# Picked rows folded in four, four, five and six banks, with masks and factors in PSUM

## What is computed

```python
# L0: a matrix per edge from the edge's features
h = relu(edge_attr @ W1 + b1); weights = (h @ W2 + b2).reshape(-1, 16, 16)
out = segment_sum(einsum('ei,eio->eo', x[src], weights), dst) + x @ root
# L1: two convolutions, 16 -> 32 -> 16
norm = dis[r] * ew * dis[c]
out = segment_sum((x @ W.T)[r] * norm[:, None], c) + b      # twice, relu between
# L2: one of 230 matrices by edge type, in a ball of curvature 0.01
msg = exp_map_zero(einsum('ei,eio->eo', h_tan[src], rel_weight[etype]) + rel_emb[etype], c)
numer = segment_sum(wl[:, None] * msg, dst); denom = segment_sum(wl, dst) + EPS
# L3: one of 90 matrices by edge type, times a scalar e of source, edge and destination
msg = einsum('ei,eio->eo', h_src, W_rel[rel_type]) * e
# after each: x = layernorm(x + out)
```

## Time and profile before

| what | us |
|---|---|
| time, median of 3 runs (lowest to highest) | 22407.31 (22362.9 to 22407.92) |
| span of the profiled execution | 16080.2 |
| the profiled execution's own time | not given with the profile |
| PE busy | 12414.4 (77%) |
| DVE busy | 12672.3 (79%) |
| ACT busy | 8008.6 (50%) |
| POOL busy | 11959.0 (74%), and idle between two gathers with nothing to wait for: 3579.0 |

### The profile page before, as it was taken

One profiled execution on the slowest core, in us unless ns is written; L12 is line 12 of the kernel. 1 busy time (PEld: TensorE's weight loads), 2 busy tenths in 40 slices (PEclk: granted clock), 3 DMA queues, 4 the chain that ended last, 5 costly groups with the idle time before them and its releaser, 6 DMA issues.

```text
span 16080.2 us, 197886 instructions
## 1 busy us (share of the span) xinstructions
PE 12414.4 (77%) x62964; PEld 11204.4 (70%) x62964; DVE 12672.3 (79%) x13275; ACT 8008.6 (50%) x6941; POOL 11959.0 (74%) x12266
## 2 busy tenths in 40 slices
PE   6777777777599999599999488888888377777774
PEld 5555555555599998599999377777777376766764
DVE  7777777777577777477777589899989599999996
ACT  1111111111466666466666377777777255555552
POOL 6777777777777777677777677777777577777776
PEclk8888888888799999799999688898888577777776
DMA  1111111111122221122221122222222222222221
GB/s 37 28 27 27 28 28 27 28 28 26 33 40 39 40 39 37 28 40 39 40 39 38 37 48 50 50 51 50 50 47 48 44 61 62 63 60 63 61 62 37
DMA packets 811074, 675.53 MB, mean 42 GB/s; under 512 B 420924, under 2 KB 729500, under 8 KB 810500
## 3 DMA queue, kind: packets, MB, share of 16 engines
q1 hardware_dynamic: 419012, 545.90, 11.4%
q0 software_dynamic: 392000, 128.94, 9.3%
HBM read 507.78 MB, written 166.09 MB: 42 GB/s over the span
## 4 chain that ended last, share of the span: by engine, by line
POOL 57%; issue 20%; DVE 8%; DVEq 8%; PE 6%; DMA 1%; ACT 0%; POOLq 0%; SPq 0%; ACTq 0%
POOL deep L637 54%; DVE big L1292 6%; PE PS L855 5%; DVEq L1040 4%; DVEq L1297 3%; POOL deep L646 3%; DVE sml L1561 0%; DVEq L1232 0%; DVE acc L1229 0%; DMA wgt<-in_edge_weight 0%; DVEq L1286 0%; DVE sml L1553 0%; DVE acc L1566 0%; DVE sml L1554 0%; DVE sml L1558 0%
## 5 line engine op out<-in xcount | busy, mean ns | idle before, releaser
L637 POOL DMA_INDIRECT deep<-table,idx x11750 | 11475.0, 977 | 3824.8 <-issue 3579.0
L797 PE MATMUL PS<-tparts,hot 125*128 125x400 f32 x22000 | 4163.7, 350 | 482.7 <-DVE big L1451 305.4
L797 PEld LDWEIGHTS PS<-tparts,hot 125*128 125x128 f32 x22000 | 4078.7, 192 | 567.4 <-DVE big L1451 387.1
L1292 DVE TENSOR_TENSOR big<-PS,deep 128x768 f32<-128x768 f32 (+4 forms) x2750 | 2984.7, 1085 | 1082.2 <-DMA deep<-table,idx 515.5
L855 PE MATMUL PS<-tparts,rhot 125*128 125x426 f32 (+1 forms) x9000 | 2302.2, 428 | 527.7 <-DVE big L1292 293.8
L855 PEld LDWEIGHTS PS<-tparts,rhot 125*128 125x128 f32 x9000 | 2177.8, 246 | 616.3 <-DVE big L1292 320.7
L944 ACT ACTIVATE hot<-deep,ones_col 128x1536 fp32r<-128x1536 bf16 x1000 | 1447.6, 1472 | 1464.7 <-PE PS L797 1424.8
L754 PE MATMUL PS<-w0b_sb,big 128*128 128x256 f32 x6250 | 1826.1, 437 | 428.4 <-DVE big L1292 390.1
L754 PEld LDWEIGHTS PS<-w0b_sb,big 128*128 128x128 f32 x6250 | 1342.2, 222 | 933.7 <-DVE big L1292 475.0
L869 PE MATMUL PS<-wx,hot 115*128 115x272 f32 x12500 | 1726.1, 293 | 311.1 <-DVE big L1292 311.1
L1275 DVE TENSOR_REDUCE acc<-big 128x64 f32<-128x1024 f32 (+2 forms) x1875 | 1940.6, 1035 | 18.3
(11 more groups left out here) (281 smaller groups left out, 9713.7 us busy)
## 6 DMA issues: line engine op xcount, KB each, us to landing
wide<-edge_types SPq DMA_DIRECT2D x250, 800.0 KB, 6.1
deep<-table,idx POOLq DMA_INDIRECT x11750, 2.4
wide<-pick_codes SPq DMA_DIRECT2D x250, 352.0 KB, 3.5
running<-msg SPq DMA_DIRECT2D x250, 212.5 KB, 2.1
running<-msg SPq DMA_DIRECT2D x250, 200.0 KB, 2.0
running<-msg SPq DMA_DIRECT2D x125, 400.0 KB, 2.5
wide<-in_edge_attr SPq DMA_DIRECT2D x125, 200.0 KB, 2.5
tabo<-pick_codes SPq DMA_DIRECT2D x125, 160.0 KB, 4.6
```

The costliest lines, as they stand in the source:

```text
L637: pool.indirect_dma_start(g[:, j, 0:GW[l]], None, tab_dram[l][:, :], bass.IndirectOffsetOnAxis(ap=idx[:, s, j:j + 1], axis=0)).then_inc(ga ...
L797: last = pe.matmul(o, poneh[0:NQ, m, c], tparts[0:NQ, k, m * JC:m * JC + JC], start=m == 0 and k == 0, stop=m == BK - 1 and k == 1)
L1292: dve.tensor_tensor(products(j), matv(l, j, n), xs, ALU.mult).then_inc(mats_free, 1)
```

## The change

- PK becomes 0, 12, 12, 5, 6. Each pass now has its own fold: BK is 4, 4, 5 and 6 banks for passes 1 to 4, with JR 25, 25, 20 and 17 nodes in a bank. Codes and `rsel` are made and stored for pass 1 (shared with 2), 3 and 4 apart.
- Passes 1 and 2 pick in groups of 3, 3, 3, 3. ACT copies the sums out (`running_out`) between the second and third group of the one-hots of the chunk two later, and DVE's L1237 goes away there.
- Pass 3 picks in groups of 3 and 2 (banks 4 to 6, then 0 and 1) and takes the matrices in groups of 3, 4, 3, 4, 3, 4, 3, 1 in banks 4 to 6 and 0 to 3 in turn. Pass 4 picks in groups of 2, 2, 2, and all its groups go round three pairs of banks.
- The scan's mask, the edge weights and the factor of the sums are written to PSUM banks 3 and 7 (slot 4 of passes 1 and 2 stays in SBUF). In passes 3 and 4 only bank 7 is used.

The diff, cut to its core:

```diff
-    PK = [0, 11, 11, 4, 5]
+    PK = [0, 12, 12, 5, 6]
-    BK, JR = 4, NJ // 4
-    JC = C * JR
+    BK = [0, 4, 4, 5, 6]
+    JR = [0, 25, 25, 20, 17]
+    JC = C * JR[1]
-    GRP = [(0, 3), (3, 3), (6, 3), (9, 2)]
-    RGRP = [[], [], [], [(0, 4)], [(0, 3), (3, 2)]]
+    GRP = [(0, 3), (3, 3), (6, 3), (9, 3)]
+    RGRP = [[], [], [], [(0, 3), (3, 2)], [(0, 2), (2, 2), (4, 2)]]
+    THREES = [(0, 3), (3, 4), (7, 3), (10, 4), (14, 3), (17, 4), (21, 3), (24, 1)]
-    BANKS = [[(2 * (k % 2), 2) for k in range(8)], None, None, [(4, 4)] + [(4 * (i % 2), 4) for i in range(6)] + [(3, 1)],
-             [(0, 3), (3, 2), (5, 2), (0, 2), (2, 2), (4, 2), (6, 2), (3, 2), (7, 1)]]
+    BANKS = [[(2 * (k % 2), 2) for k in range(8)], None, None,
+             [(4, 3), (0, 2)] + [(4, 3) if i % 2 == 0 else (0, 4) for i in range(7)] + [(3, 1)],
+             [(2 * (i % 3), 2) for i in range(9)] + [(6, 1)]]
...
+        MASK_BANK = [[None] * 5, [3, 7, 3, 7, None], [3, 7, 3, 7, None], [7] * 5, [7] * 5]
+        def mask_flat(l, s):
+            n, b = FLATC[l] * (CH + 1), MASK_BANK[l][s]
+            return mask[:, HOME[s], 0:n] if b is None else PS[:, b, 0:n]
+        def chunk_wgt(l, s):
+            b = MASK_BANK[l][s]
+            return wgt[:, s, :] if b is None else PS[:, b, 420:420 + CH]
+        fac_ps = PS[:, 7, 460:460 + CH]
...
             def run_mask(l, it, s):
-                act.wait_ge(chunks_done, it * S + (NCH * l + s + S - 1))
-                act.activation(maskv(s)[:, :, 1:CH + 1], bc_r(same[:, bass.ds(it * (S * CH) + CH * s, CH)], 17),
+                if l >= 3:
+                    act.wait_ge(scanned, it * S + (NCH * (l - 1) + s))
+                else:
+                    act.wait_ge(chunks_done, it * S + (NCH * l + s + S - 1))
+                if l in (1, 2) and MASK_BANK[l][s] is not None:
+                    act.sem_inc(act_steps, 1)
+                    act.wait_ge(loaded[s], it * (16 * LOADS[l]) + (ld_base(l) + 16 * LOADS[l]))
+                    act.copy(chunk_wgt(l, s), wgt[:, s, :])
+                act.activation(maskv(l, s)[:, :, 1:CH + 1], bc_r(same[:, bass.ds(it * (S * CH) + CH * s, CH)], FLATC[l]),
                                ACT.Identity).then_inc(masked, 1)
...
+                for i, (t0, n) in enumerate(GRP):
+                    if i == 2:
+                        if s >= 2:
+                            running_out(l, it, s - 2)
+                        elif not peeled:
+                            running_out(l, it - 1, s + S - 2)
+                        run_mask(l, it, s)
...
             def scans(l, it, s):
-                dve.wait_ge(masked, it * S + (NCH * l + s + 1))
+                if l == 0:
+                    dve.wait_ge(masked, it * S + (NCH * l + s + 1))
-                if l >= 3:
+                if l:
                     return
...
                     for s in range(S):
                         chunk_in(l, it, s)
-                        nodes_of_bank(l, it, s, iota_jr)
+                        dve.wait_ge(masked, it * S + (NCH * l + s + 1))
+                        nodes_of_bank(l, it, s, iota_jr(l, s))
...
-                        then(dve.tensor_tensor(accv(s, l)[:, 1:CH + 1, :], gatv(s, l),
-                                               wgt[:, s, :].unsqueeze(2).to_broadcast([P, CH, C]), ALU.mult))
+                        sums_free(l, it, s)
+                        then(dve.tensor_tensor(accv(s, l)[:, 1:CH + 1, :], gatv(s, l), bc_c(chunk_wgt(l, s)), ALU.mult))
...
                 if j == 5:
                     sums_free(3, it, s)
-                    then(dve.scalar_tensor_tensor(sml[:, 6, :], sml[:, 5, :], 2.0, sml[:, 4, :], ALU.mult, ALU.mult))
-                    dve.tensor_tensor(accv(s, 3)[:, 1:CH + 1, 0:C], mv, bc_c(sml[:, 6, :]), ALU.mult)
+                    dve.wait_ge(masked, it * S + (NCH * 3 + s + 1))
+                    then(dve.scalar_tensor_tensor(fac_ps, sml[:, 5, :], 2.0, sml[:, 4, :], ALU.mult, ALU.mult))
+                    dve.tensor_tensor(accv(s, 3)[:, 1:CH + 1, 0:C], mv, bc_c(fac_ps), ALU.mult)
```

More of the change, by code:

```diff
@@ L769, in _, with turn @@
             straddle(0)
-            def flip(l):
-                of, one = (flat_h, identh) if l == 1 else (flat_b, identb)
-                pe.wait_ge(flat_ready, FLIPS.index(l) + 1)
-                for r, blocks in enumerate(flip_rounds(l)):
-                    if r:
-                        pe.wait_ge(flip_sb, flip_base(l) + r)
+            def turn(what, l):
+                y = TURNS.index((what, l))
+                of, one = (flat_h, identh) if what == "codes" else (flat_b, identb)
+                pe.wait_ge(flat_ready, y + 1)
+                for r, blocks in enumerate(flip_rounds(y)):
+                    if r or (y and what == "codes"):
+                        pe.wait_ge(flip_sb, flip_base(y) + r)
                     for b, (c0, n) in enumerate(blocks):
@@ L909, in root_of, with turn @@
                 act.activation(to, of, ACT.Sqrt).then_inc(ev[done], 1)
-            def flip(l):
-                to = flip_h if l == 1 else flip_b
-                for r, blocks in enumerate(flip_rounds(l)):
-                    act.wait_ge(flip_psum, flip_base(l) + r + 1)
+            def turn(what, l):
+                y = TURNS.index((what, l))
+                to = flip_h if what == "codes" else flip_b
+                if what == "codes" and y:
+                    act.wait_ge(flip_st, 32 * y)
+                for r, blocks in enumerate(flip_rounds(y)):
+                    act.wait_ge(flip_psum, flip_base(y) + r + 1)
                     for b in range(0, len(blocks), 4):
@@ new lines, in pick_chunk @@
+            def pick_chunk(l, it, s, peeled):
+                y = PICKED.index(l)
+                act.wait_ge(rows_in[s], it * 16 + (row_base(l) + 16))
+                code = rows_h[:, HOME[s], :]
+                for m in range(BK[l]):
+                    last = act.activation(pdist[:, m, :], code[:, 0:NPK * P], ACT.Abs, bias=negbank[:, m:m + 1])
+                last.then_inc(rows_used, 1)
+                act.drain()
+                for i, (t0, n) in enumerate(GRP):
[5 more added lines that the diff above has]
+                        run_mask(l, it, s)
+                    act.wait_ge(picks, it * (S * NGR) + (NGR * (y * NCH + s) + i + 1))
+                    c = slice(t0 * P, t0 * P + n * P)
+                    act.activation(poneh[:, :, c], pdist[:, :, c], ACT.Relu, bias=ones_col[:, 0:1],
+                                   scale=-1.0).then_inc(poneh_ready, 1)
+                act.drain()
@@ L986, in one_hots @@
                 act.wait_ge(rows_in[s], it * 32 + (row_base(l) + 32))
[L987 to L988 removed]
+                rdist, rhot, oneh = rdists[l - 3], pick_hots(l), type_hots(l)
+                for m in range(BK[l]):
+                    act.activation(rdist[:, m, :], rcodes[:, HOME[s], 0:w], ACT.Abs, bias=negbank[:, m:m + 1])
                 for h in range(halves):
@@ L1437, in gcn_pass @@
                 y = PICKED.index(l)
-                then(dve.tensor_copy(iota_jr, iota_f[:, 0:JR]))
+                for s in range(2):
+                    dve.memset(maskv(l, s)[:, :, 0], 0.0)
+                    dve.tensor_copy(iota_jr(l, s), iota_f[:, 0:JR[l]])
+                dve.drain()
+                dve.sem_inc(ev["banks_set"], 1)
                 def pick_sum(s, i):
```

268 lines of the change are left out of this document (155 added, 113 removed).

## The result

The change took 23,696.81 us (median of 4 runs, 23,613.02 to 23,708.81) against 22,407.61 before: a ratio of 1.057, 95% interval 1.055 to 1.059. Slower, as forecast, but by 1,289 us and not 255, and far outside the range. The profiled run took 23,613.02 us with a span of 23,611.3: the time is the span and 1.7 us. So the 6,327 us that the prediction left unexplained hardly lie outside a span; the 16,080 us shown before look like those of an execution unlike the timed ones.

What follows compares the result with a forecast made beforehand. POOL was taken to pace passes 1, 2 and 4 and about tie with DVE in pass 3. Terms 50 + 300 - 105 + 10 = +255 us gave 22,662 us, range 22,180 to 22,900.

Steps and rivals of the forecast that it cites:

- the 6,327 us: Whole kernel: the gap between the traced span of 16080 us and the median of 22407, taken as unchanged by the change.
- +50: Passes 1 and 2: the loop through PE and DVE takes 18.2 us a chunk against 18.0, +50 us; bounds -25 to +125.
- -105: Pass 4: DVE's own 25.0 us a chunk plus some waits, against 25.8 before, -105 us; bounds -150 and -50.
- +300: Pass 3: DVE's 27.4 us plus a 2.3 us wait for PE's picks, against 27.2, +300 us; bounds +210 and +375.
- The rest: +10: Outside the chunk loops: codes made three times are covered by DVE's waits; first blocks and one table fill cost +10 us.
- rival B: POOL's gathers bind the timed runs at 1.80 us each; 500 fewer save 900 us, time 21,330; chance 0.12.
- Operands in PSUM: DVE's weights, factors and masks moved to PSUM: costed at nothing, the weight product still 0.94 us.
- C: The missing time is PE's, everything at 1.2 GHz: 23,500 to 23,950 us; chance 0.05.
- A: Pass 3: PE stays at 2.4 GHz through the 50 matmuls, so slightly faster, put at 22,300 us; chance 0.18.
- D: Nothing comes through: POOL's rate and the loops cancel, 22,407 us; chance 0.06.

## Why the prediction was wrong

**The step that failed** is "What the 6327 us are, no view shows. I take them as unchanged". They lie in the span, in all five passes, on some chips and not on others, and go away where no indirect DMAs run (pass 3) and mostly where their runs are broken. And they do change: the changed kernel adds 1,257 us in the passes. That this too needs the long runs of gathers is shown by the pauses, with which the change is 1,125 us faster and not 1,276 slower. How it comes about is read from counts and not tested by itself: matmuls beyond some 70 in a run of gathers wait until its end, and then 20 more take 4 us. By the medians over all chunks 61 matmuls were left for the rest in pass 3 before, and are 81 now: the rest grows by 4 us, the run shrinks by one gather, and 2.6 us stay. In pass 4 some 12 become 44 (11.6 us of rest and not 5.8), in passes 1 and 2 some 10 become 21. The sign of a different execution was there: POOL with 0.30 us between gathers, 1.25 us each, against 1.80 if the missing time is spread over them. What delays PE's signals, and PE itself in pass 0, stays open.

**The sum, where its ground held.** On the chip of the fast pace passes 1 and 2 took 18.06 us a chunk of POOL's gathers against 17.99 (18.2 forecast; DVE's own chunks were 18.3), pass 4 took 24.53 against 25.74 (25.0 forecast), and pass 3, without its gathers, 29.8 us of DVE's (29.7 forecast). That is +18, -151 and some +340 against the terms +50, -105 and +300. That 29.8 comes so near is in part luck: DVE waited 198.6 us for the picks' block in 124 chunks, 1.6 us each and not 2.3, so the rest of its chunk was 28.2 us and not 27.4 (waits, pass 3 of the run without gathers):

```profile
DVE big L1391 <- PE PS L916: 198.6, 151, 1.8
```

"The rest: +10" was too small. The span of that run is 357 us over the 16,080, not 218. After pass 1 POOL's last gather and its first of the node rows lie 51 us apart and not 7: once it is no longer the bound it is chunks ahead, and each pass ends by emptying what lies behind it. Passes 1, 2 and 4 end so, 44 or 45 us each, which is most of the difference. The changed kernel whole was not timed on that chip. Two slips are in the prediction's numbers: the bounds of its terms add up to +460 and not +490, and passes 1 to 4 have 8,125 gathers after the change and not 7,625 (rival B, 12 us); neither moves a verdict.

**Operands in PSUM** cost DVE nothing and gave it nothing, as forecast: the weight product took 0.94 us with its weights in SBUF, and takes 939 ns now.

```profile
L1568 DVE TENSOR_TENSOR acc<-deep,PS 128x400 f32<-128x400 f32 x98 | 92.0, 939 | 17.9 <-issue 17.9
```

**The rivals.** C gave 23,500 to 23,950 us, and the time fell into it for another reason: the clock was 0.88 and not 0.5 in passes 1 and 2, and is low where PE stands still (with POOL pausing it is 0.97 there). B had the missing time in the right place, POOL's runs, with the wrong sign: no gather got longer (947 ns on average), and 500 fewer of them bought less than what the change added. A and D ask for a change that PE hardly feels.

## What to carry to other kernels

Compare the time of the profiled execution, or its span, with the timed runs before anything else; where they differ by a quarter, terms read from the trace are of another machine, and the missing time must get a bound of its own. Where waits run in a circle, set each wait against the record of the instruction that should have ended it: where microseconds lie between them, no instruction's work explains the time. Before you call records missing, compare the page's count with the program's, and before you call instructions late, look whether the instruction queues move anything. Where a pass mixes long runs of indirect DMAs with an engine of many small instructions, break the runs (here after 6, until they have landed) and time it on more than one chip.

## What the runs showed of the hardware

- One program took 16,069 us on one chip and 22,386 to 22,976 us on four others. Without indirect DMAs in it, a pass took the same on both kinds (3,694 and 3,696 us); with a pause after every 6 of them the whole program did to within 4% (20,272 against 19,569 and 19,917 us).
- On the slow kind PE made a median of 68 to 77 matmuls (with their weight loads) in a run of gathers wherever it had that many to make, in 16 us as in 42 (63 in the longest runs of all, 58 us). In passes 1 and 2 of after DVE took up one group a chunk late, having stood idle a median 7.9 us with the group recorded as done, mostly until 2.3 to 2.5 us after the run's last gather. Why, and why one chip is free of it, stays open.
- The Trainium skill (Runtime: NRT & Kernel Launch, Instruction fetch mechanics) says that each engine's sequencer fetches its instructions through a DMA queue of its own, in blocks of 16 KiB (256 instructions), and that crossing into the next block is mostly hidden. The trace of after agrees as far as it shows: 26 packets of some 16 KB on one instruction queue, and none on any of them in 2,800 us of pass 1 in which PE lost time.

```profile
q14 instruction: 155, 1.27, 0.0%
q8 instruction: 26, 0.43, 0.0%
```

- With 64 columns and not 400 a matmul of PE took the same 0.216 us, at a granted clock of 0.50 and not 0.88.
